# Turning layer norm halves and q/k stacks by DMA transposes instead of TensorE transposes and VectorE copies

## The reference, cut to what matters

```python
x = x + _layernorm(_L0_attn_ref(_layernorm(x), W_dkv, b_dkv, W_dq, b_dq, ...))   # 16 heads of 32, all rotary
x = x + _layernorm(_L0_ffn_ref(_layernorm(x), SU_ug, SU_dp, ..., W_up, W_gate, W_down))

# attention: c_kv = x @ W_dkv + b_dkv; c_q = x @ W_dq + b_dq          (512 -> 128)
#   v = c_kv @ W_uv + b_uv; q = rope(c_q @ W_qr + b_qr); k = rope(x @ W_kr + b_kr)
#   softmax(q k^T / sqrt(32)) @ v @ W_o + b_o
# ffn: Walsh-Hadamard transform of x * SU_ug, up and gate (512 -> 2048), silu(gate) * up,
#   Walsh-Hadamard transform of (that * SU_dp), down (2048 -> 512)
```

## Time and profile before

| | |
|---|---|
| time, median of 3 runs | 2209.04 us (2207.55 to 2211.0) |
| the profiled execution: time | 2212.41 us |
| the profiled execution: span | 2210.6 us |
| granted TensorE clock, mean | 0.967 |
| PE busy | 2022.2 us (91%) |
| DVE busy | 1379.2 us (62%) |
| ACT busy | 1166.3 us (53%) |
| POOL busy | 938.4 us (42%) |

### The profile page before, as it was taken

How to read it: one execution, slowest core, us unless ns; L and a number is a source line. 1 busy time by engine, 2 the same in 40 slices (tenths; PEclk the granted TensorE clock), 3 DMA queues, 4 the chain that set the end, 5 groups by cost and what they waited for, 6 DMA issues and landing times.

```text
span 2210.6 us, 63619 instructions
## 1 busy us (share of the span) xinstructions
PE 2022.2 (91%) x26376; PEld 1493.7 (68%) x26376; DVE 1379.2 (62%) x2269; ACT 1166.3 (53%) x1757; POOL 938.4 (42%) x961
## 2 busy tenths in 40 slices
PE   1479888999999999999999999999999999999998
...
PEclk8689999999999999999999999999999999999999
...
GB/s 154 221 76 77 91 25 20 51 95 100 94 97 92 93 87 96 89 116 78 90 105 88 97 92 100 90 97 87 83 102 99 86 97 104 75 102 115 135 144 134
DMA packets 85257, 214.08 MB, mean 97 GB/s; under 512 B 17632, under 2 KB 18784, under 8 KB 83936
## 3 DMA queue, kind: packets, MB, share of 16 engines
...
## 4 chain that ended last, share of the span: by engine, by line
PE 84%; DVE 8%; issue 5%; ACT 2%; POOL 1%; DMA 0%; SPq 0%; POOLq 0%; DVEq 0%; ACTq 0%
PE ps L781 30%; PE ps L804 15%; PE ps L714 5%; PE ps L752 5%; PE ps L736 5%; PE ps L694 5%; PE ps L770 4%; PE ps L592 3%; PE ps L704 3%; PE ps L757 2%; PE ps L661 2%; DVE mx L1247 2%; PE ps L725 1%; DVE nr L1265 1%; PE ps L641 1%
## 5 line engine op out<-in xcount | busy, mean ns | idle before, releaser
L1376 POOL TENSOR_TENSOR pr<-p,pr 128x512 f16<-128x512 f32 x256 | 296.4, 1158 | 553.7 <-ACT p L950 546.1
L1247 DVE TENSOR_REDUCE mx<-ps 128x2 f32<-128x1024 f32 x256 | 311.9, 1222 | 175.0 <-PE ps L714 174.5
L944 ACT ACTIVATE pr<-ps,exp_scale 128x1024 f16<-128x1024 f32 x256 | 285.0, 1113 | 215.4 <-PE ps L736 215.1
L781 PEld LDWEIGHTS ps<-x2T,gate_w 128*128 128x128 f16 x6144 | 365.0, 99 | 38.4 <-issue 5.9
L781 PE MATMUL ps<-x2T,up_w 128*128 128x128 f16 x6144 | 389.6, 220 | 0.0
L781 PE MATMUL ps<-x2T,gate_w 128*128 128x128 f16 x6144 | 389.5, 220 | 0.0
L804 PE MATMUL ps<-room 128*128 128x512 f16 x1536 | 380.5, 384 | 6.1 <-ACT room L991 3.2
L781 PEld LDWEIGHTS ps<-x2T,up_w 128*128 128x128 f16 x6144 | 360.2, 98 | 33.4 <-issue 11.1
L981 ACT ACTIVATE room<-ps,half_gate 128x256 f32<-128x256 f32 x256 | 120.7, 475 | 306.5 <-PE ps L781 306.3
L1260 DVE TENSOR_TENSOR pr<-ps,pr 128x512 f16<-128x512 f32 x256 | 175.4, 685 | 153.2 <-ACT ps L955 153.1
L1404 POOL TENSOR_TENSOR room<-room 128x256 f16<-128x256 f32 x256 | 174.1, 681 | 220.0 <-ACT room L986 220.0
(11 more groups left out here) (188 smaller groups left out, 2879.3 us busy)
## 6 DMA issues: line engine op xcount, KB each, us to landing
room<-down_mid SPq DMA_DIRECT2D x256, 512.0 KB, 3.3
...
x2T<-in_W_gate SPq DMA_DIRECT2D x5, 1024.0 KB, 5.3
gate_w<-in_W_down SPq DMA_DIRECT2D x4, 1024.0 KB, 7.9
```

What stands on the lines that cost most here:

```text
L781: mm = nc.tensor.matmul(ffn_ps[i % 2][:, col:col + P], weights[:, j // 4, kt, pw, j % 4 * P:(j % 4 + 1) * P], x2T[:, px, kt, t * P:(t + 1) ...
L944: nc.scalar.activation(pr[:, U % 2, 0].rearrange("p (j h) q -> p j (h q)", j=2), work[k], ACT.Exp, scale=exp_scale[:, 0:1]).then_inc(p_hi. ...
L1247: nc.vector.tensor_reduce(mx[:, 2 * tp:2 * tp + 2, h], work[k], AX.X, ALU.max).then_inc(sm_freed.sem, 1)
L1376: nc.gpsimd.tensor_tensor(lo, p32[:], hi, ALU.subtract).then_inc(p_low.sem, 1)
```

## The change

The 8 transposes and the copy of each `ln1` and `ln2`, and the 16 transposes and the copy of each `stk`, are taken out. SP issues one DMA transpose in their place (`ln1`, `ln2`: 128 x 1024 halves; `stk`: 128 x 2048 halves), from SBUF to SBUF. `tok` gets 128 columns per token and head in place of 96 (zeros behind, and the constant rows for k), `kT` and `qT` are laid out tile by tile (`t h n` in place of `h s`), and what reads them follows. The waits on `ln1_freed`, `ln2_freed` and `sk_freed` become waits on the DMA semaphores `ln1_in`, `ln2_in` and `stack_in`. `ORDER`, `FRONT` and `UPPER` are written anew. `nr` is gone: the reciprocal is written to `nsc`.

```diff
@@ ORDER, cut: PE around stk.2 and stk.3 of before, smax.2.0, smax.3.0, smax.0.0@1, c.1@1 and gate.0
-        st.6 down.1@-1 smax.1.7 gate.3@-1 up.3@-1 ln2.3@-1 gate.4@-1 st.7 mrow.1 av.6 down.2@-1 up.4@-1 stk.2.0
-        gate.5@-1 stk.2.1 st.8 av.7 down.3@-1 smax.2.0 up.5@-1 down.4@-1 st.9 gate.6@-1 av.8 smax.2.1 up.6@-1
+        st.6 up.2@-1 smax.1.7 down.1@-1 gate.3@-1 st.7 up.3@-1 mrow.1 gate.4@-1 av.6 down.2@-1 st.8 up.4@-1 av.7
+        smax.2.0 gate.5@-1 down.3@-1 up.5@-1 st.9 av.8 smax.2.1 gate.6@-1 up.6@-1 st.10 av.9 smax.2.2 down.4@-1
...
+        st.13 av.12 proj.3 smax.2.6 gate.9@-1 down.7@-1 av.13 st.14 up.9@-1 smax.2.7 gate.10@-1 up.10@-1 st.15 av.14
+        down.8@-1 mrow.2 gate.11@-1 down.9@-1 av.15 st.16 up.11@-1 smax.3.0 gate.12@-1 down.10@-1 st.17 av.16 smax.3.1
+        up.12@-1 gate.13@-1 st.18 down.11@-1 av.17 smax.3.2 up.13@-1 gate.14@-1 c.1@1 st.19 down.12@-1 av.18 smax.3.3
...
+        proj.0@1 up.16@-1 smax.3.6 down.15@-1 st.22 av.21 gate.17@-1 up.17@-1 smax.3.7 gate.18@-1 up.18@-1 st.23 av.22
+        mrow.3 down.16@-1 gate.19@-1 down.17@-1 st.24 up.19@-1 av.23 smax.0.0@1 gate.20@-1 down.18@-1 up.20@-1 st.25
...
+        down.26@-1 up.28@-1 v.1@1 smax.1.0@1 gate.29@-1 st.1@1 down.27@-1 o.0 av.0@1 smax.1.1@1 av.1@1 up.29@-1 st.2@1
+        down.28@-1 o.1 smax.1.2@1 gate.30@-1 av.2@1 up.30@-1 st.3@1 down.29@-1 gate.31@-1 o.2 up.31@-1 smax.1.3@1
+        av.3@1 down.30@-1 smax.1.4@1 gate.0 st.4@1 up.0 o.3 smax.1.5@1 av.4@1 gate.1 down.31@-1 up.1 st.5@1 proj.2@1
@@ ORDER, SP
+        wl.2@-1 ln2.3@-1 wl.3@-1 stk.2.0 stk.2.1 wl.4@-1 wl.5@-1 xl.0@1 wl.6@-1 xl.1@1 wl.7@-1 wl.8@-1 xl.2@1 ln1.0@1
+        wl.9@-1 ln1.1@1 xl.3@1 stk.3.0 stk.3.1 wl.10@-1 wl.11@-1 ln1.2@1 wl.12@-1 ln1.3@1 wl.13@-1 wl.14@-1 wl.15@-1
+        wl.16@-1 wl.17@-1 stk.0.0@1 stk.0.1@1 fe.1@-1 wl.18@-1 wl.19@-1 wl.20@-1 wl.21@-1 wl.22@-1 wl.23@-1 wl.24@-1
+        rl.0 wl.25@-1 rl.1 stk.1.0@1 stk.1.1@1 wl.26@-1 fe.2@-1 wl.27@-1 wl.28@-1 wl.29@-1 wl.30@-1 oe.0 rl.2 wl.31@-1
+        ln2.0 oe.1 rl.3 wl.0 ln2.1 oe.2 wl.1 ln2.2 oe.3 fe.3@-1
@@ FRONT, SP and POOL, their beginnings
+        xl.0 xl.1 lda.0 lda.1 lda.2 lda.3 lda.4 xl.2 ln1.0 lda.5 ln1.1 xl.3 ldx.0 ldx.1 ln1.2 ldx.2 ldx.3 ldx.4 raw.0
+        ln1.3 ldx.5 raw.1 ldx.6 raw.2 ldx.7 raw.3 ldx.8 raw.4 stk.0.0 stk.0.1 ldx.9 raw.5 ldx.10 stk.1.0 stk.1.1
+        xs.0 xs.1 xn.0 xn.1 xs.2 aall xn.2 xs.3 asl.0 asl.1 asl.2 asl.3 asl.4 asl.5 asl.6 asl.7 asl.8 asl.9 asl.10
+        asl.11 xn.3 dall cut.0 cut.1 proj.0 cut.2 tok.0 cut.3 proj.1 tok.1 fall low.0 low.1 cut.4 low.2 low.3 low.4
@@ SP
+            def turn(dst, part, t, done):
+                sp.dma_start_transpose(dst[:, :, :, t * P:(t + 1) * P].rearrange("p a k n -> p (a k) n"),
+                                       nhl[:, part].rearrange("p a n -> p (a n)")).then_inc(done.sem, 16)
+            def ln1(b, t):
+                if t == 0:
+                    sp.wait_ge(*pj_filled.at(b - 1, NG - 1))
+                    sp.sem_inc(sp_turns, 1)
+                sp.wait_ge(*x_lo.at(b, t))
+                sp.sem_inc(sp_turns, 1)
+                turn(xT, 0, t, ln1_in)
+            def ln2(b, t):
+                sp.wait_ge(*f_filled.at(b - 1, (t + 1) * NJ // 2 - 1))
...
+                sp.wait_ge(*y_lo.at(b, t))
+                sp.sem_inc(sp_turns, 1)
+                turn(x2T, 1, t, ln2_in)
+            def stk(b, g, w):
+                sp.wait_ge(*st_filled.at(b, 8 * g - 9))
+                sp.sem_inc(sp_turns, 1)
+                sp.wait_ge(*tk_lo.at(b, 2 * g + w))
+                sp.sem_inc(sp_turns, 1)
+                sp.dma_start_transpose((kT, qT)[w][:, g % 2].rearrange("p t h n -> p (t h) n"),
+                                       tok[:, w].rearrange("p t h d -> p (t h d)")).then_inc(stack_in[w].sem, 16)
@@ PE: transposes(), ln1, ln2 and stk are taken out
             def smax(b, g, n):
...
                 if n == 0:
-                    pe.wait_ge(*sk_freed.at(b, 2 * g + 1))
+                    for w in range(2):
+                        pe.wait_ge(*stack_in[w].at(b, 16 * g + 15))
...
-                    mm = nc.tensor.matmul(work[k][:, i, :], qT[0:STACK, g % 2, h, t * P:(t + 1) * P], kT[0:STACK, g % 2, h, :],
+                    mm = nc.tensor.matmul(work[k][:, i, :], qT[0:STACK, g % 2, t, h, :], kT[0:STACK, g % 2, :, h, :],
@@ PE, st
-                        mm = nc.tensor.matmul(work[k][:, j, hh * HALF:(hh + 1) * HALF], kT[:, g % 2, 2 * j + hh, kt * P:(kt + 1) * P],
-                                              qT[:, g % 2, 2 * j + hh, qh * HALF:(qh + 1) * HALF], start=True, stop=True)
+                        mm = nc.tensor.matmul(work[k][:, j, hh * HALF:(hh + 1) * HALF], kT[:, g % 2, kt, 2 * j + hh, :],
+                                              qT[:, g % 2, 2 * qh:2 * qh + 2, 2 * j + hh, :], start=True, stop=True)
@@ PE: c.1 and proj wait on ln1_in, gate on ln2_in; ACT: xn waits on ln1_in, yn on ln2_in, proj on stack_in
-                sc.wait_ge(*ln1_filled.at(b, t - 1))
+                sc.wait_ge(*ln1_in.at(b, 16 * t - 1))
@@ DVE: ln1, ln2 and stk are taken out; smax.g.0 waits on neg_max of the group before
```

More of the change, by code:

```diff
@@ L65 @@
[L65 to L74, removed]
@@ L78 @@
     """,
     ACT="""
[L80 to L83, removed]
-        mrow.2 hid.10@-1 fo.0@-1 hid.11@-1 xn.2@1 norm.3 tanh.12@-1 exp.16 exq.16 exr.16 hid.12@-1 tanh.13@-1 exp.17
@@ L95 @@
+        hid.25@-1 mrow.0@1 exq.31 exr.31 tanh.26@-1 tanh.27@-1 hid.26@-1 exp.0@1 exq.0@1 v.0@1 exr.0@1 norm.7
+        hid.27@-1 tanh.28@-1 v.1@1 hid.28@-1 exp.1@1 exq.1@1 exr.1@1 oe.0 exp.2@1 exq.2@1 exr.2@1 tanh.29@-1 hid.29@-1
+        tanh.30@-1 yn.0 oe.1 exp.3@1 exq.3@1 exr.3@1 hid.30@-1 tanh.31@-1 yn.1 oe.2 yl.3@-1 exp.4@1 exq.4@1 exr.4@1
+        tanh.0 hid.31@-1 norm.0@1 hid.0 yn.2 oe.3 tanh.1 exp.5@1 exq.5@1 exr.5@1 hid.1 fe.3@-1 yn.3
     """,
     DVE="""
-        smax.1.6 gelu.2@-1 smax.1.7 mtok.1 ln2.3@-1 low.6 gelu.3@-1 low.7 stk.2.0 gelu.4@-1 stk.2.1 norm.1 smax.2.0
```

329 lines of the change are left out of this document (138 added, 191 removed).

## The result

The changed kernel takes 2119.5 us (median of 4 runs, 2115.26 to 2123.53) against 2210.0 for the one before on the same chip (4 runs, 2207.55 to 2211.15): ratio 0.9592, 95% interval 0.957 to 0.9613. The forecast was 2148, its own range 2130 to 2170, the range 2095 to 2290. The profiled execution took 2118.2 us, its span is 2116.4.

What follows compares the result with a forecast made beforehand. PE was taken as the bound outside the front. Removed transposes -72.6, stalls +12 and front 0 sum to -60.6 us: 2151.8 profiled, 2148 against the runs; range 2095 to 2290, likeliest case 2130 to 2170.

Steps and rivals of the forecast that it cites:

- The bound: PE, busy 91%, sets the time from 438 us to the end; a microsecond off its list is one off the time.
- What is removed: PE transposes of stacks and layer norm tiles: 11.1 us an iteration, 66.6 in six, 6.0 in the rest, 72.6 in all.
- VectorE and the small waits: Fewer DVE copies free PSUM slots earlier; 0.9 us an iteration can go, 3.5 at most; counted at nothing, 21 kept for range.
- The price P: Time of a pair of stack DMA transposes: 2.5 fixed, 2 x 2.7 transfer, 0.4 issue, 8.3 us, taken as 8.5.
- rival 4: DMA turns a stack's 16 blocks one after another, each at its own price: 2324 or 2616 us; chance 0.07.
- The window and the stall: PE has 8.0 us of steps before smax.g.0 needs the pair; mean stall 0.6 us, 20 times, 12 us.
- P - 7.6: Stall in group 3 before smax.3.0, where the pair starts 0.4 us late: 0.9 us.
- The weights behind the pair: In SP's queue wl.10 lands 10.9 us after st.15, down.10 due at 10.8: level, nothing counted; wl.4, wl.18 have 10 us and more.
- Layout: Moving operands of smax and st become 4 or 2 runs of 128 columns instead of one; no difference taken.
- Front and rest: Front: c.1 4 to 9 us late against work removed, taken as 0, 10 either side; rest: 6.0 us of transposes removed.
- Rival 1: Transposes hide whole (P up to 8) and PE's small waits go with the copies: 2136 to 2105 us; chance 0.12.
- Rivals 2 and 3: Pair stalls PE: P 9.5 to 11.4 gives 2166 to 2204, chance 0.15; from 11.6 slower, 2324 at 17.4, 0.30 with rival 4.

Runs made afterwards that it cites:

- e3: The changed kernel's code with the lists of the kernel before, less the steps taken out, both kinds of transpose by DMA: 2195.9 us.
- e8: The kernel before with nothing removed and mrow.0 moved two steps later, behind up.26 and st.31: 2194.6 us.
- e11: The changed kernel with mrow.0 put back right behind gate.26, its place in the kernel before: 2138.6 us.
- e6: The changed kernel with every q stack turned twice, the second time after the first has landed: 2287.1 us.
- e1: The kernel before with only the layer norm tiles turned by DMA, stacks still on PE, order of before: 2207.8 us.
- e5: The changed kernel with up.2 moved back ahead of the loop's turn: 2149.6 us.
- e13: The kernel before in its own order, no DMA transposes, most turning work left out in the loop (one PE transpose each, zeros for copies): 2158.7 us.

## Why the prediction was right, and where it was right by luck

**The bound.** PE set the time before and after. But "a microsecond off PE's list is a microsecond off the time, if nothing new makes PE wait" carried its condition too lightly: e3 takes the same steps off and gives 13 of 2209 us.

**What is removed: 11.1 us an iteration.** An iteration is 226.3 us (forecast 232). Busy PE fell by 13.6 over the four iterations compared (232.8 to 219.2). 11.1 is the transposes; the other 2.5 is the clock, which in these four iterations fell six times before (four turns, two mrow.0) and once after. L641 and L704 are gone, as said.

**VectorE and the small waits.** The 0.9 us at L641 is gone as said. The 2.2 us at mrow I had in the earlier trace rows as "issue" and took for part of the 3.5 us "of idle but the turn" that I did not count. In the trace of before VectorE's last write to mtok, the negative maxima that this mrow turns, ends 0.1 us ahead of that mrow. It was a step placed too early, and e8 gets 14.6 us from its place alone. This is the term mis-sized at zero: with the clock and what follows from it, e11 gives it 4.3 us an iteration and 19 in the whole kernel. In their place came 1.5 us an iteration at av.14, where PE waits for VectorE; the prediction has no such wait, and "frees PSUM slots earlier" does not cover it.

**The price P.** 8.4 to 8.5 to the landing in three of the four pairs of group 2, 7.9 in the mean of twelve; near the 8.5 forecast, and from a wrong split, so in part by luck. In the median tiles land in 3.7 (xT) and 4.7 us (x2T) (3.9 forecast), stacks in 4.7 (kT) and 5.9 (qT) (5.2), a packet takes about 28 ns (21) (19.3% more of 16 engines over 920 us, the added weight pieces taken out, for 102,000 packets more), and SP's issue 2 us, not 0.4. The Trainium skill (VectorE: DVE Perf Modes, section The three transpose paths) gives 1309 ns for a block by this path, by an estimate 21 us for the 16 blocks of a stack if each had its own; the trace has 4.7 and 5.9 us, 0.29 and 0.37 a block, so rival 4 falls. A single block no run has. The 261 GB/s of the prediction stand in the Trainium skill (DMA: Bandwidth & Descriptors) in section Latency and other measured facts, not in Bandwidth; the pair did not come near the 5.3 us that went with them, but took 6.8 to 9.0.

**The window and the stall.** 8.0 us and a slope of 1 hold for group 2 in both the changed kernel and e6. Group 3, for which the prediction has P - 7.6, has 9.0: between its pair and smax.3.0 stands the wait of 1.5 us at av.14, which is not in the sum. The stall of three pairs was 0.4 us an iteration, not 1.8: pairs of group 0 hid whole, those of group 3 but for 0.2 us once. That is 1.4 us an iteration to the good, and the wait at av.14 that helped to hide a pair takes 1.5 itself.

**The weights behind the pair.** Forecast level, measured 0.9 us an iteration, but not where it was looked for: down.10 does not wait, and down.18, whose piece was said to have "10 us and more", waits in three of four iterations. wl.18 is issued 3.4 to 3.6 us after its buffer is free, behind stk.0.1 and the store fe.1. That the list, and not the price, made the sum nearly right is what e3 and e1 show.

**The turn of the loop.** Not in the sum at all. It is the wait at L781 that I had said would not be there. 3.7 and 3.6 us look like no change, but with up.2 in the old place it would be 6.5 and cost 30 us (e5).

**Layout.** No difference: smax's matmuls 0.60 us for two before and after, st's 0.61 for four.

**Front and rest.** +4.1 in the front, where 0 with 10 to either side stood; c.1 started at 78.43, 12 us later (forecast 4 to 9); the prediction's own terms, 64.5 + 1.15 + 3.9 + 7.9, make 77.5 and not its "70 to 75". smax.0.0 started at 111.90, 0.4 later. The rest gave 10.4 against 6.0 less 1.2.

**The sum.** Loop -66.6 + 10.8 forecast, -87.9 measured: 32 us, of which the clock is 15, the stall 8 and the small waits, those that went less those that came, 6; the rest is that the four iterations compared are 0.3 us longer than the mean of the six. The forecast lay 28.5 us high, outside its own range and inside the full one. The side and the removed work were right for the reason given; luck is that the errors in P's split cancelled, that a wait I had not counted hid group 3's pairs, and that clock and order, which the sum does not have, went the change's way. **Rival 1** came nearest (2136 to 2105): transposes hidden and small waits gone. I gave it 0.12 for its condition, P up to 8, and the mean pair took 7.9; of its small waits only the one at L641 went with the copies, the others went with the order. **Rivals 2 and 3** priced a stall at 20 waits of P - 8; in e6 a microsecond of P cost 39 us and not 20 (168 / 4.35), so by an estimate from it the change would have lost from P near 11, not 11.6, though it had 90 us to lose and not 72.6.

**What was not expected.** The order as a part of the change of its own: the list written anew is worth 14.1 us an iteration to the kernel with DMA transposes (e3 to changed). Of this 5.2 are waits for weights, 3.4 the turn, 1.6 mrow, 4.1 clock, less 0.2 of other waits. Single steps explain part: e5 and e11 undo 5.3 and 4.3. For the weights I read the cause in SP's queue and in slower landings; lists with nothing but those pieces spaced anew, or the transposes in another engine's queue, I did not try, so there the cause is argued from the timeline and from e13, not shown by a kernel of its own.
